# Four-layer graph network on one core: in layer 3 the exponent as a maximum of a copied row and a column, the division on ScalarE, the residual on GpSimd

## The chip, the cores and the metric

The kernel runs on one core of a Trainium2 chip. A core has five engines that run side by side and wait for each other through semaphores: TensorE (PE, matrix products and transposes into PSUM), VectorE (DVE), ScalarE (ACT, functions with a scale and a bias per partition), GpSimd (POOL) and SyncE (SP, which issues DMAs). Time is device microseconds (us) of one execution; the number of a kernel is the median of its runs.

## The reference, cut to what matters

Four layers follow each other on x of shape 16 batches x 512 nodes x 128 features; after each one, `x = layernorm(x + layer(x))`. The change is nearly all in layer 3, a graph attention with one head:

```python
Wh = einsum('bnf,fo->bno', h, W)
s1 = Wh @ a1;  s2 = Wh @ a2
e = s1[:, :, None] + s2[:, None, :]
e = where(e >= 0, e, 0.2 * e)
e = where(adj_matrix == 0, -inf, e)
attention = softmax(e, axis=-1)
h_prime = einsum('bij,bjo->bio', attention, Wh)
x = layernorm(x + h_prime)
```

Layer 0 is a linear recurrence of eight steps (folded into products with powers of a matrix L), layer 1 a normalised aggregation with two small products and batch norms, layer 2 a masked attention with four heads.

## The kernel before, in words

Everything stays in SBUF: m.X holds all 16 batches. Each layer is a software pipeline over batches (layer 0: pairs of batches). A step of the pipeline is a list of items per engine; an item with stage k works on batch s - k in step s. `pairs` writes out the first and last steps and runs the rest in a loop, two steps a turn. Each engine runs its list strictly in order, and an item waits for the semaphores it needs. So the order strings set the schedule. Between layers 2 and 3 the steps of both are interleaved by hand in strings called `tail`, where "E4.15" is item E4 of layer 2 for batch 15 and "3q0.0" is item q0 of layer 3 for batch 0.

Layer 3, for one batch (tile k of 128 source nodes j on the partitions, 512 target nodes i along the row):

- PE: x (4 transposes), w0 w1 (Wh and its columns times a), j (row of s2 for the masked maximum), i (row of s1, the same in all partitions), q0 to q3 (mask plus a row with minus the maximum, through the diagonals dg, in banks 4 and 5), a0 to a3 (attention times Wh, banks 6 and 7; column 0 of Wh is one, so it gives the denominator).
- DVE: m0 to m3 (maximum over the masked row of s2), c0 c1 (the row maximum e_max from it, tiles em), e0 to e3 (the exponent: bank + S2_SLOPE column + rl), d0 d1 (reciprocal), r0 to r3 (bank x reciprocal + X, into the tile r, "rc" in the trace), b (bn_stats), B (bn_aggr).
- ACT: XR, X (copies of the transposed x), W0 W1 (copies of Wh), G (four diagonals dg from the identity), L0 to L3 (relu of 0.8 (s1 + s2)), E0 E1 (exponential over two tiles each).
- POOL: copy of X into Xc for the transposes (`pool_copy`), the root of the variance and the four applications of the layernorm (`pool_norm`). SP then stores the batch (`sync`).

The leaky relu is 0.2 e + relu(0.8 e). Tiles are double buffered by the parity of the batch: rc for batch b is free when the store of batch b - 2 has landed (`stored[par]` in item r); item W waits for av (all a of batch b - 2); item a0 waits for all exponentials of its batch and for r0, r1 of the batch before. In layer 2, the item c2 (rb = bank x reciprocal) waits for y of the batch before, since rb has one buffer; S0 to S3 on POOL make half sums for D0 D1 on PE.

## Time and profile before

| | |
|---|---|
| time, median of 3 runs | 944.48 us (944.11 to 945.14) |
| the profiled execution | 941.33 us, of it a span of 939.5 us |
| busy, share of the span | PE 92%, DVE 67%, ACT 54%, POOL 43% |
| layer 3, 850 to 900 us | of 50 us: PE 48.0, DVE 46.3, ACT 41.9, POOL 28.8 |
| granted TensorE clock | 0.987 over the span, 1.00 between 800 and 900 us |

The profile gives busy times per engine, a timeline of instructions with the idle time before each and what ended it, and the chain of waits that ended last. Layer 0 fills the span to about 343 us, layer 1 to 445 us, layer 2 to 795 us, and layer 3 the rest. A share over the whole span says little here: each layer has its own pipeline and its own bound.

### The profile page before, as it was taken

What the parts mean: (1) busy time and instruction counts of PE and PEld (TensorE: products, weight loads), DVE (VectorE), ACT (ScalarE), POOL (GpSimd) and SP (SyncE); (2) the same over time, 40 slices, a digit from 0 to 9 for tenths busy, and PEclk for the clock granted to TensorE, in tenths of its full rate; (3) what the DMA queues carried; (4) which work ended last, traced back from release to release, by engine and by line L of the source; (5) the groups of instructions that cost most, each with busy time, mean ns of one, the idle gap of its engine ahead of it and who ended that gap; (6) DMA issues with size and microseconds to landing.
All of it is one profiled execution on the core that took longest, in us unless ns stands there. A gap on an engine that the chain in (4) does not pass through costs nothing. (4 is left out here: it accounts for less than half of the span.)

```text
span 939.5 us, 20538 instructions
## 1 busy us (share of the span) xinstructions
...
## 2 busy tenths in 40 slices
...
DMA packets 34249, 40.82 MB, mean 43 GB/s; under 512 B 6673, under 2 KB 17553, under 8 KB 34193
## 3 DMA queue, kind: packets, MB, share of 16 engines
...
## 5 line engine op out<-in xcount | busy, mean ns | idle before, releaser
L1678 POOL TENSOR_TENSOR half_sum<-prob 128x1024 f32<-128x1024 f32 x64 | 151.4, 2378 | 21.6 <-PE bank L1942 20.3
L1753 ACT ACTIVATE prob<-wide 128x1024 f32<-128x1024 f32 x128 | 124.2, 1023 | 38.3 <-PE wide L1934 38.1
L458 ACT CAST yT<-wide 128x512 fp32r<-128x512 f32 x48 | 28.1, 588 | 190.9 <-PE wide L862 141.9
L1822 DVE CUSTOM_DVE_ANT_0 junk<-wide,mask_ij 128x512 bf16<-128x512 f32 x128 | 82.7, 684 | 52.1 <-PE bank L1914 51.0
L1930 PE MATMUL wide<-qk_st 128*128 128x512 f32 x256 | 84.5, 435 | 3.2 <-ACT prob L1753 1.7
L1822 DVE CUSTOM_DVE_ANT_0 junk<-bank,mask_ij 128x512 bf16<-128x512 f32 x128 | 83.0, 685 | 0.0
L551 POOL TENSOR_TENSOR Xr<-Xf,Xr 128x512 fp32r<-128x512 f32 x16 | 20.4, 1291 | 140.1 <-ACT Xr L453 139.9
L1488 PEld LDWEIGHTS bank<-Wh,pr 128*128 128x128 f32 x512 | 65.2, 191 | 15.6 <-ACT pr L1341 7.0
L1488 PE MATMUL bank<-Wh,pr 128*128 128x129 f32 x512 | 68.5, 278 | 6.4 <-ACT pr L1341 5.5
L59 PE MATMUL bank<-z,L3T_hi 128*128 128x256 f32 x256 | 72.6, 284 | 1.3 <-DVE z L675 1.3
L61 PE MATMUL bank<-z,L3T_lo 128*128 128x256 f32 x256 | 72.3, 283 | 0.0
L60 PE MATMUL bank<-z,L3T_hi 128*128 128x256 f32 x256 | 72.3, 282 | 0.0
L1930 PEld LDWEIGHTS wide<-qk_st 128*128 128x128 f32 x256 | 46.4, 192 | 30.2 <-DVE mx L1822 19.2
L154 POOL TENSOR_SCALAR n_rstd<-n_aggr 128x4 f32<-128x4 f32 x31 | 7.2, 233 | 135.7 <-DVE n_aggr L147 130.3
L1952 PE MATMUL bank<-prob,v 128*32 128x512 f32 x512 | 61.6, 598 | 1.2 <-ACT prob L1753 1.2
L661 DVE TENSOR_TENSOR yT<-wide,yT 128x512 fp32r<-128x512 f32 x48 | 32.9, 686 | 31.8 <-ACT yT L458 31.8
L59 PEld LDWEIGHTS bank<-z,L3T_hi 128*128 128x128 f32 x256 | 48.7, 190 | 3.4 <-DVE z L675 2.6
L684 DVE TENSOR_TENSOR zf<-bank,G 128x256 f32<-128x256 f32 x64 | 27.0, 421 | 33.7 <-PE bank L61 32.0
L1914 PEld LDWEIGHTS wide<-qkT 32*128 32x128 f32 x128 | 12.3, 184 | 56.2 <-ACT prob L1753 29.6
L60 PEld LDWEIGHTS bank<-z,L3T_hi 128*128 128x128 f32 x256 | 48.8, 191 | 0.4
L61 PEld LDWEIGHTS bank<-z,L3T_lo 128*128 128x128 f32 x256 | 48.9, 191 | 0.0
L1377 DVE SCALAR_TENSOR_TENSOR pr<-bank,Wh,rl 128x512 f32<-128x512 f32 x64 | 44.9, 741 | 5.9 <-PE bank L1500 5.4
...
## 6 DMA issues: line engine op xcount, KB each, us to landing
...
qk_st<-neg_row SPq DMA_DIRECT2D x64, 2.0 KB
...
```

Of the source, the lines that this page charges most:

```text
L59: pe.matmul(out, stat[0], mov[0], start=start, stop=False)
L60: pe.matmul(out, stat[0], mov[1], start=False, stop=False)
L61: return pe.matmul(out, stat[1], mov[0], start=False, stop=stop)
L458: act.copy(yT[bb][i][0][:], psum_y[i][:]).then_inc(y_hi, 1)
L661: dve.tensor_tensor(yT[bb][i][1][:], psum_y[i][:], yT[bb][i][0][:].bitcast(F32), ALU.subtract).then_inc(y_lo, 1)
L1377: dve.scalar_tensor_tensor(out=pr[par][:, k], in0=bank[4 + k % 2][:], scalar=Wh[par][:, k, S2_SLOPE:S2_SLOPE + 1], in1=rl[par][:, k], op0= ...
L1488: last = pe.matmul(out_bank[h][:, t * (D + 2):t * (D + 2) + D + 1], pr[par][:, j, k * P:k * P + P], Wh[par][:, j, 0:D + 1], start=(j == 0) ...
L1678: pool.tensor_tensor(flat(half_sum[h][:]), flat(prob[bp][h][:, 0:2]), flat(prob[bp][h][:, 2:4]), ALU.add).then_inc(h_sum, 1)
L1753: act.activation(flat(prob[bp][h][:, 2 * half:2 * half + 2]), wide[half][:], ACT.Exp, scale=SCALE).then_inc(t_exp, 1)
L1822: dve.tensor_tensor_reduce(out=junk[h % 2][:], in0=ROWS[h][:], in1=m.mask_ij[:, i], scale=1.0, scalar=3.0 * MASKED, op0=ALU.add, op1=ALU.m ...
L1930: pe.matmul(bank[j][:], k_st[:, k, j * P:j * P + P], q_st[:, k], start=True, stop=True)
L1952: last = pe.matmul(ring["V0"][c, :], v[bp][:, k, c], prob[bp][h][:, k], start=(k == 0), stop=(k == NT - 1), skip_group_check=True)
```

## The change

In layer 3, the leaky relu is written as max(0.8 s1, -0.8 s2) + (mask and row) and s2 comes in as the bias of the exponential. e is then max(s1, 0.2 s1 - 0.8 s2) + s2 up to the row's own terms. The items become:

- ACT: L is gone; Z copies the s1 row from bank 1 to SBUF once per batch; E0 to E3 are four exponentials of one tile each, with the bias S2; R0 to R3 multiply bank 6 or 7 by the reciprocal into a new tile y; G is gone.
- DVE: e reads the copied row, the column S2_BEND and the bank (maximum, then addition); G (four products of the identity with em) is now on DVE; r is gone but for the last two batches; b and B have stage 3 in place of 2.
- POOL: `pool_add` adds y and X into rc, one instruction per batch with stage 4; the layernorm has stage 5 in place of 3.
- The s1 row always uses bank 1; the tile rl (and its place over qkT) is gone.
- The order strings of the transition from layer 2 to 3 change on PE, ACT, DVE and POOL.
- In layers 0 and 1, DVE's orders for the last steps of layer 0 change, its last two looped steps are written out, POOL makes the low part of batch 4 earlier, and DVE's statistics of the hidden layer start later.

```diff
-        LAST = ... "DVE": order("N z z z z A p p #a0 p #w0 p z z z z p p p p #a1 n #W0 #v0 a"),
-        LATE = ... "DVE": order("#a2 N A")}
+        LAST = ... "DVE": order("z z z z A p p #a0 p #w0 p z z z z p p p p #a1 n #W0 #v0 a"),
+        LATE = ... "DVE": order("#a2 N #a3 A")}
+        WHOLE = ... "DVE": order("h h y z z N y z z y A p p g p g g p g y z z y z z y p p g g n p p M g g a")}
...
                 if alive[2]:
                     for u in range(2):
+                        if u == 1 and isinstance(s, int) and s == groups + 1:
+                            batch_low(4, 0)
                         norm.root(pool, (s - 2 + CREDIT) * 2 + u, u)
...
-    ACT_ORDER = staged("L3:2 E0:2 W0:1 W1:1 E1:2 XR:0 G:1 L0:1 L1:1 X:0 L2:1")
-    DVE_ORDER = staged("m0:0 m1:0 d0:2 e0:1 e1:1 r0:2 m2:0 e2:1 e3:1 m3:0 r1:2 d1:2 c0:0 c1:0 r2:2 r3:2 b:2 B:2")
+    ACT_ORDER = staged("E0:2 E1:2 E2:2 W0:1 W1:1 E3:2 XR:0 Z:1 R2:3 R3:3 X:0 R0:2 R1:2")
+    DVE_ORDER = staged("m0:0 m1:0 d0:2 e0:1 e1:1 m2:0 e2:1 e3:1 d1:2 m3:0 c0:0 c1:0 G:0 b:3 B:3")
...
+    def late(b):
+        return isinstance(b, int) and b >= LAST - 1
...
+    def pool_add(pool, b, par, nth):
+        pool.wait_ge(res, after(b, NT))
+        pool.wait_ge(stored[par], (nth + 1) * 16)
+        pool.tensor_tensor(flat(r[par][:]), flat(y[par][:]), batch_flat(m.X, b), ALU.add).then_inc(summed, 1)
+
     def pool_rest(pool):
         def step(s, par, alive, nth):
             if alive[0]:
                 pool_copy(pool, s, par)
-            pool_norm(pool, s - 3, 1 - par, s if alive[0] else B - 1)
+            if alive[5]:
+                pool_norm(pool, s - 5, 1 - par, s if alive[0] else B - 1)
+            if alive[4] and not late(s - 4):
+                pool_add(pool, s - 4, par, nth - 2)
...
+            elif what == "Z":
+                act.wait_ge(s1_ps, after(b, 1))
+                act.wait_ge(e_s, after(b - 2, NT))
+                act.copy(s1[par][:], bank[1][:]).then_inc(s1_c, 1)
+            elif what == "R":
+                if late(b):
+                    return
...
+                act.activation(y[par][:, k], out_bank[h][:, t * (D + 2) + 1:t * (D + 2) + D + 1], ACT.Copy,
+                               scale=rec[par][:, k:k + 1]).then_inc(res, 1)
             elif what == "E":
-                two = flat(pr[par][:, 2 * k:2 * k + 2])
-                act.activation(two, two, ACT.Exp).then_inc(ex, 1)
+                act.activation(pr[par][:, k], pr[par][:, k], ACT.Exp,
+                               bias=Wh[par][:, k, S2:S2 + 1]).then_inc(ex, 1)
...
-                dve.scalar_tensor_tensor(out=pr[par][:, k], in0=bank[4 + k % 2][:],
-                                         scalar=Wh[par][:, k, S2_SLOPE:S2_SLOPE + 1], in1=rl[par][:, k],
-                                         op0=ALU.add, op1=ALU.add).then_inc(e_s, 1)
+                dve.scalar_tensor_tensor(out=pr[par][:, k], in0=s1[par][:],
+                                         scalar=Wh[par][:, k, S2_BEND:S2_BEND + 1], in1=bank[4 + k % 2][:],
+                                         op0=ALU.max, op1=ALU.add).then_inc(e_s, 1)
...
+            elif what == "G":
+                dve.wait_ge(e_m, after(b, 2))
+                dve.wait_ge(r_ps, after(b - 2, NT))
+                for t in range(NT):
+                    dve.tensor_scalar(dg[par][:, t], m.identb[:], em[par][:, 1, t:t + 1], None, ALU.mult).then_inc(d_g, 1)
             elif what == "d":
...
+                if isinstance(b, int) and b == LAST - 1:
+                    item(f"r{2 * k}", b, par, nth)
+                    item(f"r{2 * k + 1}", b, par, nth)
...
     def dve_last(dve, item):
+        item("b", LAST - 1, 0, LAST // 2)
+        item("B", LAST - 1, 0, LAST // 2)
...
-            tail("g2.13 S0.15 S1.15 S2.15 r.14 S3.15 g2.14", POOL_ORDER, work, None)
+            tail("g2.13 S0.15 S1.15 S2.15 S3.15 r.14 g2.14", POOL_ORDER, work, None)
...
-                 "E2.15 E3.15 f.14 3W1.0 E4.15 E5.15 e.14 E6.15 E7.15 3G.0 3L0.0 3L1.0 y.13 3XR.1 3L2.0 3L3.0 3X.1 f.15 e.15 "
-                 "3E0.0 3W0.1 3W1.1 y.14 3E1.0 3XR.2 3G.1 3L0.1 3L1.1 3X.2 3L2.1 y.15", ACT_ORDER, work, item)
+                 "E2.15 E3.15 f.14 3W1.0 e.14 y.13 E4.15 E5.15 E6.15 E7.15 3XR.1 3X.1 f.15 3Z.0 e.15 "
+                 "3E0.0 3E1.0 3W0.1 3W1.1 3E2.0 3E3.0 3XR.2 3Z.1 y.14 3X.2 3R0.0 3R1.0 y.15", ACT_ORDER, work, item)
```

The scales of the columns change with the formula, PE's items keep their sizes, and no DMA is added or removed.

The next two pieces are DVE's instructions in layer 3 behind its loop, from the last looped step on: first the kernel before. The tiles rc_4756 and rc_4757 belong to even and odd batches, so rc_4757 is batch 13 and then 15, rc_4756 batch 14; the pr rows are e of batch 15.

```order
L1393 RECIPROCAL rec_4765<-bank 128x2
L1377 SCALAR_TENSOR_TENSOR pr_4768<-bank,Wh_4750,rl_4760 128x512 x2
L1401 SCALAR_TENSOR_TENSOR rc_4756<-bank,rec_4765,X 128x128
L1377 SCALAR_TENSOR_TENSOR pr_4768<-bank,Wh_4750,rl_4760 128x512 x2
L1401 SCALAR_TENSOR_TENSOR rc_4756<-bank,rec_4765,X 128x128
L1393 RECIPROCAL rec_4765<-bank 128x2
L1401 SCALAR_TENSOR_TENSOR rc_4756<-bank,rec_4765,X 128x128 x2
L141 BN_STATS n_stats<-rc_4756 128x6 x4
L147 BN_AGGR n_aggr<-n_stats 128x2 x4
L1393 RECIPROCAL rec_4766<-bank 128x2
L1401 SCALAR_TENSOR_TENSOR rc_4757<-bank,rec_4766,X 128x128 x2
```

And the changed kernel at the same place, where rc_4732 is even and rc_4733 odd:

```order
L1418 RECIPROCAL rec_4743<-bank 128x2
L1429 SCALAR_TENSOR_TENSOR rc_4732<-bank,rec_4743,X 128x128 x2
L1397 SCALAR_TENSOR_TENSOR pr_4746<-s_row_4738,Wh_4726,bank 128x512 x4
L1418 RECIPROCAL rec_4743<-bank 128x2
L1429 SCALAR_TENSOR_TENSOR rc_4732<-bank,rec_4743,X 128x128 x2
L142 BN_STATS n_stats<-rc_4733 128x6 x4
L148 BN_AGGR n_aggr<-n_stats 128x2 x4
L142 BN_STATS n_stats<-rc_4732 128x6 x4
L148 BN_AGGR n_aggr<-n_stats 128x2 x4
L1418 RECIPROCAL rec_4744<-bank 128x2
L1429 SCALAR_TENSOR_TENSOR rc_4733<-bank,rec_4744,X 128x128 x2
```

r0 and r1 of batch 14 now stand ahead of all four e of batch 15, and the statistics of batch 13, which stood inside the loop, stand behind them.

The next two are POOL behind its loop: first the kernel before, which has the layernorm of batch 13 (rc_4757) and the roots of 14 and 15 left.

```order
L154 TENSOR_SCALAR n_rstd<-n_aggr 128x4
L156 TENSOR_TENSOR n_rstd<-n_rstd,neg_half 128x4
L182 TENSOR_SCALAR rc_4757<-rc_4757,n_aggr,n_rstd 128x128 x4
L154 TENSOR_SCALAR n_rstd<-n_aggr 128x4
L156 TENSOR_TENSOR n_rstd<-n_rstd,neg_half 128x4
```

And the changed kernel, in whose rows batch 11 comes first, with y_4735 and y_4736 the quotients from ScalarE:

```order
L183 TENSOR_SCALAR rc_4733<-rc_4733,n_aggr,n_rstd 128x128 x4
L1306 TENSOR_TENSOR rc_4732<-y_4735,X 128x512
L155 TENSOR_SCALAR n_rstd<-n_aggr 128x4
L157 TENSOR_TENSOR n_rstd<-n_rstd,neg_half 128x4
L183 TENSOR_SCALAR rc_4732<-rc_4732,n_aggr,n_rstd 128x128 x4
L1306 TENSOR_TENSOR rc_4733<-y_4736,X 128x512
```

The sum of batch 12 stands behind the layernorm of batch 11, and the sum of batch 13 behind the layernorm of batch 12.

The last two are ACT in the transition from layer 2 to layer 3, around y.14, the row with X<-rb; first the kernel before, from e.15 on:

```order
L1763 COPY denT<-bank 128x512
L1341 ACTIVATE pr_4767<-pr_4767 128x1024
L1323 COPY Wh_4750<-wide 128x2x131 x2
L175 ACTIVATE X<-rb,n_shift,n_rstd 128x128 x4
L1341 ACTIVATE pr_4767<-pr_4767 128x1024
L1314 CAST xTr_4751<-wide 128x512
```

And the changed kernel from e.15 on:

```order
L1792 COPY denT<-bank 128x512
L1362 ACTIVATE pr_4745<-pr_4745,Wh_4725 128x512 x2
L1344 COPY Wh_4726<-wide 128x2x131 x2
L1362 ACTIVATE pr_4745<-pr_4745,Wh_4725 128x512 x2
L1335 CAST xTr_4727<-wide 128x512
L1349 COPY s_row_4738<-wide 128x512
L176 ACTIVATE X<-rb,n_shift,n_rstd 128x128 x4
```

y.14 has moved behind the last exponential of batch 0, the cast XR.2 and the copy Z.1.

## Rows read from the trace of the kernel before

**Rows 1.** Busy time by window, layer 3: window, length, then busy us per engine.
```profile
850.00:900.00 50.00, 48.03 (x323) 37.29 (x321) 46.34 (x168) 41.90 (x83) 28.81 (x41) 1.00 0.11 31
```
**Rows 2.** Timeline of PE, layer 3: start us, us, engine line op, [idle before <-releaser].
```profile
819.04 0.66 PE L1450 MATMUL wide<-ident,Xc 128*128 128x128 f32 x4
820.08 1.16 PE L1488 MATMUL bank<-Wh,pr 128*128 128x129 f32 x8 [0.38 <-ACT pr L1341]
...
922.04 2.05 PE L1488 MATMUL bank<-Wh,pr 128*128 128x129 f32 x16 [0.84 <-ACT pr L1341]
```
**Rows 3.** Timeline of DVE over one step of layer 3, b of one batch to the next.
```profile
811.77 0.87 DVE L141 BATCH_NORM_STATS2 n_stats<-rc 128x6 f32<-128x128 f32 x4
...
819.03 0.15 DVE L1383 SCALAR_TENSOR_TENSOR em<-Wh,mx 128x4 f32<-128x4 f32 x1
819.22 0.16 DVE L1388 SCALAR_TENSOR_TENSOR em<-mx,em 128x4 f32<-128x4 f32 x1
819.50 0.61 DVE L1401 SCALAR_TENSOR_TENSOR rc<-bank,rec,X 128x128 f32<-128x128 f32 x2
820.14 0.87 DVE L141 BATCH_NORM_STATS2 n_stats<-rc 128x6 f32<-128x128 f32 x4
```
**Rows 4.** Timeline of POOL: an addition of layer 2, then layer 3.
```profile
801.45 1.27 POOL L1684 TENSOR_TENSOR rb<-rb,X 128x512 f32<-128x512 f32 x1 [6.69 <-DVE rb L1835]
...
818.25 0.61 POOL L1267 COPY Xc<-X 128x512 f32 x1 [0.25 <-POOL rc L182]
821.77 0.19 POOL L154 TENSOR_SCALAR n_rstd<-n_aggr 128x4 f32<-128x4 f32 x1 [2.91 <-DVE n_aggr L147]
...
823.28 3.12 POOL L182 TENSOR_SCALAR rc<-rc,n_aggr,n_rstd 128x128 f32<-128x128 f32 x4 [0.21 <-POOL n_rstd L156]
```
**Rows 5.** Timeline of DVE, layers 0 and 2, narrow windows.
```profile
351.90 1.17 DVE L182 TENSOR_SCALAR X<-zf,n_aggr,n_rstd 128x128 f32<-128x128 f32 x1 [1.66 <-POOL n_rstd L156]
352.99 1.32 DVE L182 TENSOR_SCALAR X<-zf,n_aggr,n_rstd 128x128 f32<-128x128 f32 x1
802.50 0.24 DVE L1383 SCALAR_TENSOR_TENSOR em<-Wh,mx 128x4 f32<-128x4 f32 x1
```
**Rows 6.** Timeline of POOL at the first two of these.
```profile
351.71 1.26 POOL L556 TENSOR_TENSOR Xa<-X,Xa 128x512 fp32r<-128x512 f32 x1
352.94 1.28 POOL L556 TENSOR_TENSOR Xa<-X,Xa 128x512 fp32r<-128x512 f32 x1
```
**Rows 7.** Instructions of line 182: duration ns min/median/max.
```profile
L182 DVE TENSOR_SCALAR X<-zf,n_aggr,n_rstd x64: 333/341/1323, 106.1 to 354.5; 128x128 f32<-128x128 f32 x32, 128x128 f32 x32
```
**Rows 8.** Groups of instructions, 850 to 900 us: count, busy us, mean ns, idle us.
```profile
L1330 ACT ACTIVATE rl<-wide,Wh 128x512 f32<-128x512 f32 x23 | 14.7, 697 | 0.0
```
**Rows 9.** Timeline of the end, DVE and POOL.
```profile
922.43 0.87 DVE L141 BATCH_NORM_STATS2 n_stats<-rc 128x6 f32<-128x128 f32 x4
931.63 0.61 DVE L1401 SCALAR_TENSOR_TENSOR rc<-bank,rec,X 128x128 f32<-128x128 f32 x2 [1.20 <-DMA out_dram<-rc]
...
925.54 3.12 POOL L182 TENSOR_SCALAR rc<-rc,n_aggr,n_rstd 128x128 f32<-128x128 f32 x4 [0.21 <-POOL n_rstd L156]
```
**Rows 10.** Timeline of PE at the seam of layers 0 and 1.
```profile
326.85 0.39 PE L59 MATMUL bank<-z,L3T_hi 128*128 128x256 f32 x1 [0.96 <-DVE z L675]
353.04 0.50 PE L59 MATMUL wide<-AhT_hi,Xa 128*128 128x512 f32 x1 [1.50 <-POOL Xa L556]
357.94 0.49 PE L59 MATMUL bank<-agT,W1T 128*128 128x512 f32 x1 [1.84 <-DVE agT L650]
```
**Rows 11.** Timeline of PE, DVE and ACT at the seam of layers 2 and 3.
```profile
785.82 1.92 PE L1952 MATMUL bank<-prob,v 128*32 128x512 f32 x16
...
791.82 3.33 PE L1942 MATMUL bank<-half_sum,ones_hd 128*32 128x512 f32 x16 [3.64 <-POOL half_sum L1678]
800.55 0.69 DVE L1835 TENSOR_TENSOR rb<-bank,rec 128x512 f32<-128x512 f32 x1 [0.60 <-ACT X L175]
798.77 1.65 ACT L175 ACTIVATE X<-rb,n_shift,n_rstd 128x128 f32<-128x128 f32 x4
```

More of the change, by code:

```diff
@@ L80, in setup_constants, with pairs @@
     m.AhT = [sb("AhT_hi", [P, NT, N], F32R), sb("AhT_lo", [P, NT, N], F32R)]
-def pairs(eng, steps, depth, step, first=0, last=None):
+def pairs(eng, steps, depth, step, first=0, last=None, loop_to=None):
     def alive(s):
@@ L92, in pairs @@
         step(s, s % 2, alive(s), s // 2)
-    with eng.Fori(lead // 2, steps // 2) as r:
+    loop_to = steps if loop_to is None else loop_to
+    with eng.Fori(lead // 2, loop_to // 2) as r:
         for parity in range(2):
             step(r * 2 + parity, parity, [True] * depth, r)
-    for s in range(steps, steps + depth - 1 if last is None else last + 1):
+    for s in range(loop_to, steps + depth - 1 if last is None else last + 1):
         step(s, s % 2, alive(s), s // 2)
@@ L587, in _ @@
             pairs(pool, groups, 5, step)
-            for b in range(4, 6):
-                batch_low(b, b - 4)
+            batch_low(5, 1)
             pool.wait_ge(la_x_lo, after(5, 1))
@@ L805, in step, with hidden_statistics @@
                                                  op1=ALU.subtract).then_inc(v_Ah, 1)
-            pairs(dve, groups, 5, step)
+            pairs(dve, groups, 5, step, loop_to=groups - 2)
+            def hidden_statistics(b):
+                for c in range(CH):
+                    dve.wait_ge(la_h_sb, after(b, CH, c + 1))
+                    dve.bn_stats(L1.st1[:, c, bass.ds(b, 1)].rearrange("p a n -> p (a n)"),
+                                 Hb[:, bass.ds(b, 1), c].rearrange("p a n -> p (a n)")).then_inc(la_h_st, 1)
             def aggregate_step(s, par, alive, nth):
-                early = isinstance(s, int) and s < 4
-                if alive[1] and not early:
+                if alive[1]:
                     aggregate_low(s - 1, 1 - par)
                 if alive[2]:
-                    b = s - 2
-                    for c in range(CH):
-                        dve.wait_ge(la_h_sb, after(b, CH, c + 1))
-                        dve.bn_stats(L1.st1[:, c, bass.ds(b, 1)].rearrange("p a n -> p (a n)"),
-                                     Hb[:, bass.ds(b, 1), c].rearrange("p a n -> p (a n)")).then_inc(la_h_st, 1)
-            pairs(dve, B, 5, aggregate_step)
+                    hidden_statistics(s - 2)
+            for b, behind in ((4, (0,)), (5, (1, 2)), (6, (3, 4)), (7, (5, 6)), (8, (7,))):
+                aggregate_low(b, b % 2)
+                for k in behind:
+                    hidden_statistics(k)
+            pairs(dve, B, 3, aggregate_step, first=10)
         @block.tensor
@@ L1138, in staged, with layer3 @@
     return [(word.split(":")[0], int(word.split(":")[1])) for word in text.split()]
-def layer3(nc, own, m, bank, out, rl1_at, ready):
+def layer3(nc, own, m, bank, out, ready):
     at = [172352]
@@ L1167, in layer3 @@
     onesb = over("onesb", [P, P], BF16)
-    rl = [over("rl0", [P, NT, N]), nc.alloc_sbuf_tensor_at("rl1", [P, NT, N], F32, offset=rl1_at)]
+    y = [over(f"y3{k}", [P, NT, D]) for k in range(2)]
+    s1 = [over(f"s1_row{k}", [P, N]) for k in range(2)]
     mx = [over(f"mx3{k}", [P, NT]) for k in range(2)]
@@ L1211, in half, with rest_of @@
         return bank[4 + k] if is_batch(b, 0) else bank[0] if k else bank[3]
-    def s1_bank(b):
-        return bank[4] if is_batch(b, 0) else bank[1]
+    def late(b):
+        return isinstance(b, int) and b >= LAST - 1
+    def rest_of(b, k):
+        return (late_res, (b - LAST + 1) * NT + k) if late(b) else (res, after(b, NT, k))
     def in_order(item, items):
@@ L1402, in item @@
                                          scalar=rec[par][:, k:k + 1], in1=tile_of(m.X, b, k),
-                                         op0=ALU.mult, op1=ALU.add).then_inc(res, 1)
+                                         op0=ALU.mult, op1=ALU.add).then_inc(late_res, 1)
             elif what == "b":
-                dve.wait_ge(res, after(b, NT))
+                if late(b):
+                    dve.wait_ge(*rest_of(b, NT))
+                else:
+                    dve.wait_ge(summed, after(b, 1))
                 norm.statistics(dve, b + CREDIT, par, r[par])
@@ L1446, in item @@
                 if is_batch(b, 1):
-                    pe.wait_ge(*ready["second wide"])
+                    pe.wait_ge(*ready["first two"])
                 pe.wait_ge(wh_c, after(b - 1, 2))
@@ L1485, in item @@
                 for j in range(NT):
[L1486 to L1487 removed]
+                    if one_by_one and j >= 1:
+                        pe.wait_ge(ex, after(LAST, NT, j + 1))
                     last = pe.matmul(out_bank[h][:, t * (D + 2):t * (D + 2) + D + 1],
```

96 lines of the change are left out of this document (41 added, 55 removed).

## The prediction

> **What bounds the kernel now.** I read the busy times by window first, then the timeline of one step of layer 3 on each engine, then the two seams between layers, and last the chain at the end.
>
> In layer 3 no engine is far from full [rows 1]: PE 48.0 of 50 us, DVE 46.3, ACT 41.9. A step is one batch. From the start of a0 at 820.08 to the start of a0 of batch 14 at 922.04 [rows 2] there are 12 steps, so 8.50 us each. PE is idle in each step before a0, 0.30 to 0.38 us (0.38 in the row shown), until ACT has done the double exponential. Ahead of that it waits for W1 before x, which does not change. So PE could go at about 8.50 - 0.34 = 8.16 us if the exponentials came sooner.
>
> DVE is nearly as full: from b of one batch at 811.77 to b of the next at 820.14 [rows 3] are 8.37 us without a gap, and behind it DVE waits a little for j. That is the engine that the change relieves, and it moves work to POOL, which works 28.8 of 50 us.
>
> **The change part by part.**
>
> *Seam of layers 0 and 1.* PE stands three times [rows 10]. At 326.85 it waits 0.96 us for z, since the statistics N stand ahead of z on DVE. They move into the step before (M), where DVE waits for PE anyway: -0.9. At 353.04 PE waits for the low part of batch 4, which POOL makes at 351.71 [rows 6] behind two roots. It now stands between them: the wait of 1.50 us goes. At 357.94 it waits 1.84 us for agT, which stood on DVE behind the four applications A and four statistics. It now stands ahead of both. The time goes whole, since PE stands nowhere else near: 4.3, and with the pipeline's refill of some 0.1 to 0.2 at each of them 4.6 us. If one of the inputs is late for another reason, 3. I take -4.6.
>
> *Seam of layers 2 and 3.* PE waits 3.64 us at 791.82 for the last half sum, and the 16 products behind the wait take 3.33 us, where 16 of the same width at 785.82 take 1.92 [rows 11]. The half sum S3.15 now stands ahead of r.14, and D0.14 ahead of t2.15. The wait and the slow products go: up to 3.64 + 1.41, less 0.2 for the s1 row's product and the exponentials that move: -4.8. Against it stands y.14. At 798.77 it ran between the two exponentials of batch 0 [rows 11], and c2.15 on DVE waits for it (0.60 us at 800.55). Now it stands behind E2.0, E3.0, XR.2 and Z.1, four instructions of ScalarE at some 0.6 to 0.7 us each [rows 8]: 2.6 later. Behind c2.15 on DVE are queued m2.1 and m3.1, for which j.2 on PE waits, and then a1.0 and q0.1, so PE stands at j.2. y.15 also comes ahead of the exponentials of batch 1. Together +3.0. The sum of this seam is -1.8, between -4.8 (y.14 costs nothing) and +1.
>
> *Relu, division, residual in the steady loop, if nothing gets in the way.* ACT loses four relus of 0.70 us [rows 8] and four diagonals, gains one copy of a row and four products of 128 columns, and its exponentials come one tile at a time. Then a0 waits for a single tile behind W1, and the idle time before a0 goes: 8.16 us a step. I cost e at the same time as before, since it still reads one bank, one SBUF tile and one column. DVE loses four r, two of which take 0.64 us from 819.50 to b at 820.14 [rows 3]: -1.28, leaving 7.09. It gains four G of 128 bf16 columns. No row shows one; bounds are c0's 0.15 (4 columns) and r's 0.32 (128 columns): 0.6 to 1.3 us a step, so 7.7 to 8.4. POOL gains one sum of 128x512, as that at 801.45: 1.27 us [rows 4]. Its own chain per batch, counted from the start of b: root at 821.77 - 820.14 = 1.63, the four applications from 3.14 to 6.26, then 0.25 (as before the copy at 818.25), the sum from 6.51 to 7.78, and b of the next batch may start. 7.8 is under 8.16.
>
> *DVE and POOL at the same moment.* The trace shows them in each other's way. At 351.71 POOL begins an instruction of 1.26 us, ending at 352.97. DVE's tensor_scalar of 128 columns, issued at 351.90, ends at 353.07, 0.10 after it. The next is issued at 352.99, POOL's next runs from 352.94 to 354.22, and DVE's ends at 354.31 [rows 5, 6]; the median of these instructions is 0.34 us [rows 7]. Of the kind of c0, one at 802.50 takes 0.24 in place of 0.15 [rows 3, 5], and it ends at 802.74, where POOL's sum from 801.45 ends at 802.72 [rows 4]. In the loop before, c0 and c1 fell into POOL's idle time, and no instruction of G's kind was there. The Trainium skill says the same in "SBUF — State Buffer", section "Who interferes with whom": a DVE instruction with two SBUF inputs, or in a two-port mode, and a GpSimd instruction lock each other out for a whole instruction. By that rule, the trace agrees.
>
> Where does c0 fall now? Counted from b: 819.03 - 811.77 = 7.26 in the row, less two r (0.64), is 6.62. The sum on POOL runs from 6.51 to 7.78. So c0 is held until 7.78. c1 follows 0.19 later and G 0.28 after that [rows 3], at 8.25. By then POOL's copy has begun (7.78 + 0.25 = 8.03, for 0.61 [rows 4]), so G starts at 8.64, and four take 0.6 at the 0.15 that I take for one (bounds 0.15 and 0.32): b at 9.24 (to 9.9). As b starts POOL's next chain, this repeats in every step, whatever its length: 9.24 us in place of 8.16. If G does not need what POOL holds, it goes from 8.25 on, and the step has 8.9 to 9.5 all the same. The rule of "VectorE: DVE Perf Modes", section "The TRN2 errata", gives 58 + FD/4 cycles, an estimate of 0.09 us for one G; the step would have 9.0.
>
> From a0.1 to a0.14 are 13 steps: two before the first sum meets a c0, then eleven. 13 x (8.16 - 8.50) = -4.4, and 11 x (9.24 - 8.16) = +11.9: +7.5.
>
> *The end.* Before, b of batch 13 starts at 922.43, its applications end at 928.66, and r0 of batch 15 waits for the landed store until 931.63 [rows 9]; from there to the end of the span are 7.87. From a0.14 at 922.04 it is 17.46 in all. Now b has stage 3, and POOL does the sum of batch 13 only behind the applications of batch 12. b of batch 12 starts about 1.3 us behind a0.14 (0.8 without the collision). From there: 6.26 to the end of its applications, 2.97 for the store (931.63 - 928.66), and only then may r0 of batch 14 write, which stands ahead of e of batch 15: 9.2. Then r0 and r1 (0.6), four e, d1, r2 and r3 of 14: 4.2 more, of which the e are some 0.7 each. b of batch 13 starts at 13.4 to 14; 6.26 and 2.97 again to r0 of batch 15: 22.9. I take 22.1, since the e may overlap with the store's last part. The end is 7.87 behind. Sum 1.3 + 22.1 + 7.87 = 31.3 against 17.46: +13.8. Nothing hides it: all other engines have finished by then.
>
> **The sum.** -4.6 - 1.8 + 7.5 + 13.8 = +14.9. The profiled execution took 941.33, so 956.2; the median is 3.15 above the profiled execution, so 959.4 us.
>
> **The rivals.**
>
> *The engines do not collide in the loop* (the sum and c0 miss each other, or c0 is not held). For it: only one c0 in the trace is held, and it was a tenth of a microsecond. Against: the margin from 6.51 to 7.78 is wide, and DVE's next instruction would fall in it too. Then the step has 8.16 and the end 0.5 less: -4.6 - 1.8 - 4.4 + 13.3 = +2.5, 947.0 us.
>
> *It is faster.* The same, and PE fills entirely: with ACT emptier W1 comes sooner, the further stall before x goes, and y.14 costs nothing. From x at 819.04 to a0 at 820.08 are 1.04 us [rows 2], of which x itself needs 0.5, so 0.54 a step with no stall at all: 13 x 0.54 = 7.0. -4.6 - 4.8 - 7.0 + 13.3 = -3.1, 941.4 us. It decides if DVE's step stays under 7.9, which needs every c and G free of POOL. Against it: the end alone takes all that back.
>
> *The end is milder.* If the stores land well before r0.14 and r0.15, the end costs some 5 in place of 13.8, with the collision in the loop: 950.6 us. The chain of applications, store and r at 931.63 speaks against it.
>
> *Collision with a slow G* of 0.32: 9.9 a step, +7.3 more, 966.7 us.
>
> **How the numbers follow.** Forecast 0.55 (own range 953 to 965), no collision 0.2, milder end 0.1, slow G 0.07, faster 0.08. What a measurement can tell from no change is 0.2%, 1.9 us. No collision at 947.0 with 3 us around lies half over 946.4 and half in or under it. So slower 0.83, same 0.08, faster 0.09. The range, 945 to 966, leaves out the faster case and the far ends.
>
> **What would show it.** In the changed kernel's profile: PE without idle time at 326, 353 and 358 us; D of batch 15 without a wait, and PE idle at j.2 instead. In the loop, a0 to a0 at 9.2 us, PE's busy share in layer 3 falling to about 7.9 of 9.2, and em and dg instructions on DVE ending together with POOL's sum and copy. At the end, two waits of DVE for a store, at r of batch 14 and of 15. I am wrong if a0 to a0 stays under 8.5, or if DVE does not wait for a store ahead of batch 15's e.

## The result, and the profile after

The changed kernel takes 957.11 us (median of 4 runs, 955.41 to 957.61), the kernel before on the same chip 944.3. The ratio is 1.0134, 95% interval 1.0116 to 1.0152: slower by 1.2 to 1.5%. The forecast was 959.4. By the medians the change costs 12.8 us.

The profiled execution took 957.17 us, with a span of 955.3; before, 941.33 and 939.5. The one before was 3 us faster than its median and this one was not, so the difference of the two spans, 15.8 us, holds some 3 us of spread between executions. It falls into four parts, read from three places that both traces have: the residual c2.12 late in layer 2 (the rb row on DVE), the start of a0 of batch 1, and the start of a0 of batch 14.

| stretch | before | after | difference | forecast |
|---|---|---|---|---|
| start to c2.12 (seam 0/1) | 751.32 | 746.39 | -4.9 | -4.6 |
| c2.12 to a0.1 (seam 2/3) | 60.2 | 62.1 | +1.9 | -1.8 |
| a0.1 to a0.14 (13 steps) | 110.5 | 114.4 | +3.9 | +7.5 |
| a0.14 to the end | 17.5 | 32.4 | +14.9 | +13.8 |

The rows of these places, first DVE of the kernel before, then DVE and PE of the changed kernel (timelines: start us, us, engine line op):

```profile
751.32 0.69 DVE L1835 TENSOR_TENSOR rb<-bank,rec 128x512 f32<-128x512 f32 x1
```
```profile
746.39 0.69 DVE L1864 TENSOR_TENSOR rb<-bank,rec 128x512 f32<-128x512 f32 x1
...
808.53 1.16 PE L1519 MATMUL bank<-Wh,pr 128*128 128x129 f32 x8
...
922.93 2.05 PE L1519 MATMUL bank<-Wh,pr 128*128 128x129 f32 x16 [0.53 <-ACT pr L1362]
```

Busy times by window of the changed kernel. The three stops of [rows 10] are gone: PE is busy 50.00 of 50 us in both windows of the first seam. Layer 3, against [rows 1], has less on PE (46.6 for 48.0) and on ACT (33.5 for 41.9), more on POOL (33.4 for 28.8), and as much as before on DVE.

```profile
300.00:350.00 50.00, 50.00 (x312) 45.97 (x311) 27.73 (x93) 14.29 (x31) 11.08 (x13) 1.00 0.04 6
350.00:400.00 50.00, 50.00 (x216) 40.28 (x215) 26.78 (x45) 28.86 (x48) 20.17 (x16) 1.00 0.00 0
...
850.00:900.00 50.00, 46.62 (x307) 35.34 (x306) 46.12 (x159) 33.54 (x74) 33.35 (x44) 1.00 0.11 31
```

*The second seam*, PE, DVE and ACT of the changed kernel, against [rows 11] (L1959 t3.15, L1971 D of batch 15, L1519 a0.0, L1864 c2.15, L176 y.13 and y.14, L1782 the exponentials E4.15 and E5.15):

```profile
776.56 2.04 PE L1959 MATMUL wide<-qk_st 128*128 128x512 f32 x4 [2.66 <-ACT prob L1782]
...
787.15 1.92 PE L1971 MATMUL bank<-half_sum,ones_hd 128*32 128x512 f32 x16
...
797.94 2.06 PE L1519 MATMUL bank<-Wh,pr 128*128 128x129 f32 x8 [3.84 <-DVE rb L1864]
...
797.10 0.69 DVE L1864 TENSOR_TENSOR rb<-bank,rec 128x512 f32<-128x512 f32 x1 [3.23 <-ACT X L176]
...
772.96 1.65 ACT L176 ACTIVATE X<-rb,n_shift,n_rstd 128x128 f32<-128x128 f32 x4
774.51 1.91 ACT L1782 ACTIVATE prob<-wide 128x1024 f32<-128x1024 f32 x2
...
795.31 1.65 ACT L176 ACTIVATE X<-rb,n_shift,n_rstd 128x128 f32<-128x128 f32 x4
```

D of batch 15 has no wait and takes 1.92 in place of 3.33, as forecast. But a0.0 now stands 3.84 us for c2.15, which stands 3.23 for y.14; the forecast had this stop at j.2. And there is a place that the forecast didn't have: t3.15, the last scores of layer 2, stands 2.66 us for the exponentials E4.15 and E5.15, ahead of which y.13 runs on ACT from 772.96.

*One step of layer 3*, DVE and then POOL, against [rows 3, 4]:

```profile
851.40 1.01 DVE L1403 SCALAR_TENSOR_TENSOR em<-Wh,mx 128x4 f32<-128x4 f32 x1
852.45 0.16 DVE L1408 SCALAR_TENSOR_TENSOR em<-mx,em 128x4 f32<-128x4 f32 x1
852.65 0.74 DVE L1414 TENSOR_SCALAR dg<-identb,em 128x128 bf16<-128x128 bf16 x4
853.31 0.87 DVE L142 BATCH_NORM_STATS2 n_stats<-rc 128x6 f32<-128x128 f32 x4
...
860.69 0.68 DVE L1403 SCALAR_TENSOR_TENSOR em<-Wh,mx 128x4 f32<-128x4 f32 x1
...
862.25 0.87 DVE L142 BATCH_NORM_STATS2 n_stats<-rc 128x6 f32<-128x128 f32 x4
...
850.58 1.27 POOL L1306 TENSOR_TENSOR rc<-y,X 128x512 f32<-128x512 f32 x1
851.79 0.61 POOL L1280 COPY Xc<-X 128x512 f32 x1
854.90 0.20 POOL L155 TENSOR_SCALAR n_rstd<-n_aggr 128x4 f32<-128x4 f32 x1 [2.50 <-DVE n_aggr L148]
...
856.42 3.14 POOL L183 TENSOR_SCALAR rc<-rc,n_aggr,n_rstd 128x128 f32<-128x128 f32 x4 [0.21 <-POOL n_rstd L157]
859.52 1.27 POOL L1306 TENSOR_TENSOR rc<-y,X 128x512 f32<-128x512 f32 x1
860.74 0.61 POOL L1280 COPY Xc<-X 128x512 f32 x1
```

c0 does the same work as before, on 4 columns, where it took 0.15 us. The one issued at 851.40 ends at 852.41, the one at 860.69 at 861.37; POOL's copies end at 852.40 and 861.35. G is not held: four take 0.74. From b to b are 8.94 us.

*The end*, DVE and then POOL, against [rows 9]:

```profile
923.91 0.86 DVE L142 BATCH_NORM_STATS2 n_stats<-rc 128x6 f32<-128x128 f32 x4
...
932.82 0.61 DVE L1429 SCALAR_TENSOR_TENSOR rc<-bank,rec,X 128x128 f32<-128x128 f32 x2 [7.37 <-DMA out_dram<-rc]
...
938.58 0.86 DVE L142 BATCH_NORM_STATS2 n_stats<-rc 128x6 f32<-128x128 f32 x4
...
947.43 0.61 DVE L1429 SCALAR_TENSOR_TENSOR rc<-bank,rec,X 128x128 f32<-128x128 f32 x2 [6.10 <-DMA out_dram<-rc]
...
927.03 3.14 POOL L183 TENSOR_SCALAR rc<-rc,n_aggr,n_rstd 128x128 f32<-128x128 f32 x4 [0.21 <-POOL n_rstd L157]
...
941.69 3.13 POOL L183 TENSOR_SCALAR rc<-rc,n_aggr,n_rstd 128x128 f32<-128x128 f32 x4 [0.21 <-POOL n_rstd L157]
```

DVE stands twice for a landed store, 7.37 us ahead of r0.14 and 6.10 ahead of r0.15, where before it stood 1.20. From b.12 to r0.15 are 23.5 us.

### The profile page after: what moved, and what is told of

Its sections match the earlier page's. It is cut to its first block and busy times, and to the rows that moved or that the text cites. A ratio compares the mean times of both kernels' runs of the same rounds, so it can differ in the third digit from the quotient of the medians.

```text
span 955.3 us, 20263 instructions
## 1 busy us (share of the span) xinstructions
PE 870.6 (91%) x6039; PEld 624.0 (65%) x6039; DVE 629.3 (66%) x1939; ACT 485.2 (51%) x878; POOL 420.9 (44%) x465
## 3 DMA queue, kind: packets, MB, share of 16 engines
q1 hardware_dynamic: 32816, 39.87, 17.4%
## 5 line engine op out<-in xcount | busy, mean ns | idle before, releaser
L1782 ACT ACTIVATE prob<-wide 128x1024 f32<-128x1024 f32 x128 | 124.1, 1022 | 38.5 <-PE wide L1963 38.4
L1959 PE MATMUL wide<-qk_st 128*128 128x512 f32 x256 | 84.8, 437 | 5.9 <-ACT prob L1782 4.3
L1519 PEld LDWEIGHTS bank<-Wh,pr 128*128 128x128 f32 x512 | 69.0, 201 | 14.4 <-issue 6.8
L1519 PE MATMUL bank<-Wh,pr 128*128 128x129 f32 x512 | 71.9, 288 | 4.6 <-DVE rb L1864 3.8
L1959 PEld LDWEIGHTS wide<-qk_st 128*128 128x128 f32 x256 | 46.7, 194 | 32.9 <-DVE mx L1851 18.5
L1362 ACT ACTIVATE pr<-pr,Wh 128x512 f32<-128x512 f32 x64 | 45.1, 724 | 19.7 <-DVE pr L1397 19.5
```

The costliest lines, as they stand in the source:

```text
L1362: act.activation(pr[par][:, k], pr[par][:, k], ACT.Exp, bias=Wh[par][:, k, S2:S2 + 1]).then_inc(ex, 1)
L1519: last = pe.matmul(out_bank[h][:, t * (D + 2):t * (D + 2) + D + 1], pr[par][:, j, k * P:k * P + P], Wh[par][:, j, 0:D + 1], start=(j == 0) ...
L1782: act.activation(flat(prob[bp][h][:, 2 * half:2 * half + 2]), wide[half][:], ACT.Exp, scale=SCALE).then_inc(t_exp, 1)
L1959: pe.matmul(bank[j][:], k_st[:, k, j * P:j * P + P], q_st[:, k], start=True, stop=True)
```

## The experiments

Each ratio is to the kernel before, run on the same chip; the median of the kernel before was 942.7 to 944.0 beside these runs. The changed kernel was not run beside them. So "under the changed kernel" means under its median of 957.11, measured at another time; taken from the ratios, the same gains are smaller: 10.7 us for 12.2, 8.2 for 9.7, 8.4 for 9.5 and 2.8 for 3.3. The traces stand nearer to the smaller figures, as said at each. The theory was: DVE and POOL collide at c0 in every step, and the end is a chain through two stores.

**Own buffers at the end.** Batches 14 and 15 get tiles for the result and the aggregates, where qkT lay.

```diff
-                dve.scalar_tensor_tensor(out=r[par][:, k], in0=out_bank[h][...],
+                dve.scalar_tensor_tensor(out=r_late[par][:, k], in0=out_bank[h][...],
...
-                    dve.wait_ge(stored[par], (nth + 1) * 16)
+    aggr_late = [... offset=late_at + (2 + k) * NT * D * 4 ...]
```

> The changed kernel, with a result buffer and an aggregate of their own for batches 14 and 15, so that r0.14 and r0.15 need no landed store of batches 12 and 13. Theory (the longer end is the chain of applications, store, r, twice): DVE does r0.14 right behind d0.14, b.13 starts behind the sum of batch 13, and from a0.14 to the end of the span it takes about 20 to 21 us in place of 32.4: 957.1 - 12 = 945 us (943 to 947). The loop stays at 8.96 a step. Rival (the end is long because the products and exponentials of batch 15 come late, or because b has stage 3, and the stores only happen to land there): under 4 us are gained, 953 or more.

944.92 us (943.30 to 947.16), ratio 1.0021 [0.9999, 1.0042]: 12.2 under the changed kernel, as the theory had it. From a0.14, at 920.13, to the end of the span, 941.5, are 21.4 us, 11.0 less than in the changed kernel; the rest of the difference lies ahead of a0.14, where these buffers are not used. Both waits for a store are gone; what is left ahead of b.13 is 1.55 us for POOL's sum:

```profile
922.69 0.61 DVE L1440 SCALAR_TENSOR_TENSOR r_late<-bank,rec,X 128x128 f32<-128x128 f32 x2
...
928.65 0.87 DVE L142 BATCH_NORM_STATS2 n_stats<-rc 128x6 f32<-128x128 f32 x4 [1.55 <-POOL rc L1318]
```

The edit leaves the loop as it was, and yet the collision looks different in every second step. DVE, then POOL:

```profile
849.35 0.47 DVE L1415 SCALAR_TENSOR_TENSOR em<-Wh,mx 128x4 f32<-128x4 f32 x1
849.85 0.52 DVE L1420 SCALAR_TENSOR_TENSOR em<-mx,em 128x4 f32<-128x4 f32 x1
...
848.53 1.27 POOL L1318 TENSOR_TENSOR rc<-y,X 128x512 f32<-128x512 f32 x1
```

This c0 was issued 0.82 us into the sum, as the one at 851.40 in the changed kernel was. Here it ends with the sum (849.82 and 849.80), and c1 is held by the copy in its place; there it was held through the copy. c0 takes 577 ns on average of eight (850 of nine in the changed kernel), and the eleven steps up to a0.14 take 8.82 us each in place of 8.90. What decides between the two is not shown.

**POOL's sum first.**

```diff
+            if alive[4] and not late(s - 4):
+                pool_add(pool, s - 4, par, nth - 2)
             if alive[5]:
                 pool_norm(pool, s - 5, 1 - par, s if alive[0] else B - 1)
-            if alive[4] and not late(s - 4):
-                pool_add(pool, s - 4, par, nth - 2)
```

> The changed kernel, with POOL's sum of a batch ahead of the root and the applications of the batch before it, in place of behind them. Nothing else moves. Theory (a closed loop: B on DVE releases the root on POOL, 1.5 us; applications 3.14, sum 1.27, copy 0.61 follow without a gap, c0 of DVE is held till the copy's end, then c1, G, b, B: 8.96): the sum now runs beside b and B, the copy ends before c0 is issued, c0 takes 0.15 again, and the step falls to 8.2 to 8.3, where PE bounds it: 13 x 0.65 = 8.5 us less, about 949 us (947 to 951). Rival (a step is long because DVE has G, the new e and c0 to do, and c0's duration is only idle time shown as work): within 2 us of 957.

957.35 us (955.39 to 962.01), ratio 1.0163 [1.0110, 1.0216]. No gain: the forecast of 949 fell. The trace, POOL and DVE, says why:

```profile
858.66 0.61 POOL L1280 COPY Xc<-X 128x512 f32 x1 [0.24 <-POOL rc L183]
861.13 1.27 POOL L1306 TENSOR_TENSOR rc<-y,X 128x512 f32<-128x512 f32 x1 [1.86 <-DMA out_dram<-rc]
```
```profile
857.98 0.16 DVE L1403 SCALAR_TENSOR_TENSOR em<-Wh,mx 128x4 f32<-128x4 f32 x1
858.18 0.16 DVE L1408 SCALAR_TENSOR_TENSOR em<-mx,em 128x4 f32<-128x4 f32 x1
858.37 1.11 DVE L1414 TENSOR_SCALAR dg<-identb,em 128x128 bf16<-128x128 bf16 x4
```

The sum has to wait for the store of the batch two before, which the old place hid: 1.86 us idle, and the root of the next applications stands behind it. So POOL's chain slid by about as much as was won. c0 is nearly free (0.16 here, 0.33 to 0.35 in three of the later steps), but the copy now falls on G, 1.11 for 0.74. The step is 8.67 on average of eleven (823.59 to 919.00) rather than 8.2, which wins 2.5 us on the changed kernel, and the end, with applications of batch 12 behind such a sum, gave the rest back: from b.12 at 919.80 to r0.14 at 931.03 are 11.2 in place of 8.9. So the first part of the theory held (what POOL does when c0 comes sets c0's time), and the price of the move had been left out.

**Sum and copy in four instructions each.**

```diff
-        pool.tensor_tensor(flat(r[par][:]), flat(y[par][:]), batch_flat(m.X, b), ALU.add).then_inc(summed, 1)
+        for t in range(NT):
+            last = pool.tensor_tensor(r[par][:, t], y[par][:, t], tile_of(m.X, b, t), ALU.add)
+        last.then_inc(summed, 1)
```

> The changed kernel, with POOL's sum and copy of a batch in four instructions of 128 columns each. The work and the order are the same. Theory (DVE's c0 waits for the end of the one instruction that POOL has under way): c0 takes at most 0.35 in place of up to 1.0 and no longer waits for the last of them; the step falls by 0.3 to 0.6, so 950 to 954 us. G may now meet parts of the copy, each 0.15. Rival (c0 waits for POOL's whole batch of work, or the duration comes from something else): c0 stays at 0.6 to 1.0 and the time at 957.

962.85 us (960.51 to 965.09), ratio 1.0202 [1.0153, 1.0252]: slower still, against the forecast. The edit does not leave POOL's time alone, as the expectation had it: from the start of the sum to the end of the copy are 2.64 us (863.12 to 865.76), where one instruction each took 1.83 (859.52 to 861.35). Of the 6.3 us by which the spans differ, 1.4 lie between a0.1 and a0.14, 2.7 at the end and 2.2 ahead of a0.1. POOL, then DVE:

```profile
863.12 1.69 POOL L1312 TENSOR_TENSOR rc<-y,X 128x128 f32<-128x128 f32 x4
864.76 1.00 POOL L1284 COPY Xc<-X 128x128 f32 x4
```
```profile
864.27 1.50 DVE L1410 SCALAR_TENSOR_TENSOR em<-Wh,mx 128x4 f32<-128x4 f32 x1
865.80 0.16 DVE L1415 SCALAR_TENSOR_TENSOR em<-mx,em 128x4 f32<-128x4 f32 x1
```

c0 starts at 864.27, in the third of the four sums, and ends at 865.77, when the last of four copies has ended (865.76). It was passed over at five boundaries between POOL's instructions. In the step before it was issued just ahead of such a boundary and ended with the next instruction, after 0.48. The ten steps alternate: five c0 take 1.49 to 1.69 and end with the copy, five take 0.48 to 0.49. So c0 does not always get in when the one instruction under way ends; in half of the steps it waits until POOL's whole run of instructions has ended. In the changed kernel the c0 of 851.40 comes during a sum and leaves behind the copy, too.

**G back on ScalarE.**

```diff
-    DVE_ORDER = staged("... m3:0 c0:0 c1:0 G:0 b:3 B:3")
+    DVE_ORDER = staged("... m3:0 c0:0 c1:0 b:3 B:3")
-    ACT_ORDER = staged("... E3:2 XR:0 Z:1 ...")
+    ACT_ORDER = staged("... E3:2 XR:0 G:1 Z:1 ...")
```

> The changed kernel, with the four diagonals G back on ScalarE (behind the copy XR, as in the kernel before; POOL's order stays). Theory (closed loop of 8.96 through POOL): c0 is held just as long, but the loop loses G's 0.66 between c1 and b: 8.30 a step, so about 8 us less, 949 us (947 to 951), with c0 still at 0.6 to 1.0. Rival 1 (the price is G's alone, since DVE is full): c0 falls back to 0.15 and the step to the 8.16 of PE, 947 or less. Rival 2 (ScalarE becomes late with its products and exponentials): no gain, 955 or more.

947.44 us (946.58 to 949.63), ratio 1.0047 [1.0027, 1.0067]: 9.7 under the changed kernel; between a0.1 and a0.14 the trace has 7.3 us less. The time is near to rival 1, and so is c0, which is back at 0.16 to 0.21 (187 ns on average of nine): the theory's figure of 0.6 to 1.0 was wrong. Without G's 0.66 the loop has 8.30 us at most, PE has 8.2, and the two are so near that c0 comes just as the copy ends. The step is 8.25 (808.06 to 898.83 in eleven). The run does not part G's own time from the hold, since it removes both.

**b ahead of c0, c1, G.** This run leaves G on DVE: no work is added or moved to another engine.

```diff
-    DVE_ORDER = staged("m0:0 m1:0 d0:2 e0:1 e1:1 m2:0 e2:1 e3:1 d1:2 m3:0 c0:0 c1:0 G:0 b:3 B:3")
+    DVE_ORDER = staged("m0:0 m1:0 d0:2 e0:1 e1:1 m2:0 e2:1 e3:1 d1:2 m3:0 b:3 B:3 c0:0 c1:0 G:0")
```

> The changed kernel with one move on DVE: b and B of a batch ahead of c0, c1 and G, in place of behind them. Work and all other orders stay. Theory (c0 waits because POOL's sum and copy run back to back when it comes, and stands in the loop B, root, applications, sum, copy, c0, c1, G, b, B): c0 now comes 1.2 us later, when POOL has ended its copy, and is out of the loop through b; c0 takes 0.15 to 0.3, the step falls from 8.96 to 8.2 to 8.5, 6 to 9 us less, 948 to 951 us. G can be held by POOL's root (1.03) in some steps. Rival (q0 of the next step waits for G, which comes 1.2 later, so PE stands): the step stays at 8.9 or goes up, 956 or more.

947.61 us (946.27 to 948.46), ratio 1.0045 [1.0028, 1.0062]: 9.5 under the changed kernel, G still on DVE. Its windows row, then DVE and PE of one step:

```profile
850.00:900.00 50.00, 49.52 (x333) 39.19 (x339) 46.91 (x174) 37.03 (x80) 37.69 (x49) 1.00 0.11 31
```
```profile
857.45 0.16 DVE L1403 SCALAR_TENSOR_TENSOR em<-Wh,mx 128x4 f32<-128x4 f32 x1
857.65 0.16 DVE L1408 SCALAR_TENSOR_TENSOR em<-mx,em 128x4 f32<-128x4 f32 x1
857.85 0.75 DVE L1414 TENSOR_SCALAR dg<-identb,em 128x128 bf16<-128x128 bf16 x4
...
856.66 1.16 PE L1519 MATMUL bank<-Wh,pr 128*128 128x129 f32 x8
...
864.89 1.15 PE L1519 MATMUL bank<-Wh,pr 128*128 128x129 f32 x8
```

PE has no idle time before q or a0 any more, and from a0 to a0 are 8.18 us (807.61 to 897.59 in eleven). DVE has as much to do as in the changed kernel. These 13 steps (807.61 to 913.78) take 8.2 us less than in the changed kernel. So what the steady part lost came of the loop that the hold of c0 closed: b, root, applications, sum, copy, then c0, c1 and G, and b again. The move takes c1 and G out of that loop together with c0, so their shares are not measured apart; but G's 0.66 us, which DVE still has to do, cost nothing outside it. Rival: PE would stand for G. It does not.

**The seams.** First, the kernel before with the edits between layers 0 and 1 alone:

```diff
+        WHOLE = {"PE": ORDER, "ACT": ORDER, "DVE": order("h h y z z N y ... n p p M g g a")}
+                        if u == 1 and isinstance(s, int) and s == groups + 1:
+                            batch_low(4, 0)
```

> The kernel before with only the edits at the seam of layers 0 and 1 (statistics M a step earlier, low part of batch 4 between the two roots, agT ahead of the last applications, statistics of batches 0 to 7 beside the low parts). Theory: the three stops of PE of 0.96, 1.50 and 1.84 us go with their refill, 4.6 to 4.9 us less, about 938 (the before of this chip at 942.7), ratio 0.995, and all later parts of the trace stand the same time apart as in the kernel before. Rival (part of it is taken back at the start of layer 1, where something else is late): under 2 us, ratio over 0.998.

937.86 us (936.71 to 938.45), ratio 0.9933 [0.9910, 0.9957]: 4.1 to 8.5 us less. PE is full in both windows (50.00 of 50), and c2.12 comes at 747.63, 3.7 earlier. The rival is out; whether the seam is worth 3.7, 4.9 or 6 lies inside the spread of single traces.

Next, the kernel before with one swap on POOL:

```diff
-            tail("g2.13 S0.15 S1.15 S2.15 r.14 S3.15 g2.14", POOL_ORDER, work, None)
+            tail("g2.13 S0.15 S1.15 S2.15 S3.15 r.14 g2.14", POOL_ORDER, work, None)
```

> The kernel before with one swap on POOL: the half sum S3.15 ahead of the residual r.14. Theory: the residual waits for DVE until 788.1, so the half sum runs in that wait and ends some 3.3 us earlier; the idle 3.64 of PE ahead of D.15 and its slow 3.33 in place of 1.92 go, 3.5 to 4.8 us less, ratio about 0.996. Rival (the normalisation y.14 and c2.15 behind it are then what a0.0 waits for, since their chain starts at the residual, which now comes later): 0 to 1.5 us less.

938.51 us (937.07 to 940.90), ratio 0.9939 [0.9918, 0.9960]: 3.8 to 7.7 us less, so the rival (0 to 1.5) is out. D.15 on PE has 0.33 of its 3.64 idle left, and its normal 1.92:

```profile
790.09 1.92 PE L1942 MATMUL bank<-half_sum,ones_hd 128*32 128x512 f32 x16 [0.33 <-POOL half_sum L1678]
```

Last, the changed kernel with y.14 moved:

```diff
-                 "E2.15 E3.15 f.14 3W1.0 e.14 y.13 ... f.15 3Z.0 e.15 "
-                 "3E0.0 3E1.0 3W0.1 3W1.1 3E2.0 3E3.0 3XR.2 3Z.1 y.14 3X.2 3R0.0 3R1.0 y.15"
+                 "E2.15 E3.15 f.14 3W1.0 e.14 y.13 ... f.15 3Z.0 e.15 y.14 "
+                 "3E0.0 3E1.0 3W0.1 3W1.1 3E2.0 3E3.0 3XR.2 3Z.1 3X.2 3R0.0 3R1.0 y.15"
```

> The changed kernel with the normalisation y.14 on ScalarE moved ahead of the exponentials of batch 0, behind the copy e.15. Theory (c2.15 on DVE, and a0.0 on PE behind it, wait for y.14: 3.23 and 3.84 us in the changed kernel): c2.15 goes at about 793.7 in place of 797.1, a0.0 follows the last exponential, 3 us less, 954 us. Rival (the root of batch 14, or y.15 behind it, is late anyway): under 1 us less.

953.81 us (952.55 to 954.15), ratio 1.0104 [1.0080, 1.0128]: 3.3 less. DVE and PE:

```profile
794.21 0.69 DVE L1864 TENSOR_TENSOR rb<-bank,rec 128x512 f32<-128x512 f32 x1
```
```profile
795.05 1.13 PE L1519 MATMUL bank<-Wh,pr 128*128 128x129 f32 x8
```

c2.15 waits for nothing, a0.0 comes 2.9 earlier and at full clock.

On top of that, y.13 was moved too:

```diff
-                 "... e.14 y.13 E4.15 E5.15 E6.15 E7.15 ..."
+                 "... e.14 E4.15 E5.15 y.13 E6.15 E7.15 ..."
```

> The changed kernel with y.14 ahead of the exponentials of batch 0 (953.8), and y.13 on ScalarE behind E4.15 and E5.15 of layer 2 in place of ahead of them. Theory (the missing gain of the second seam: y.13, 1.65 us, stands ahead of E4.15, so the last scores product t3.15 stands 2.66 us on PE, PE's granted clock falls to 0.60 behind it and the four products take 2.04): the wait falls to 0.5 to 1.2 us, the products take 1.2, q0.0 comes 2 to 3 us earlier than its 789.25, and so does a0.1; about 951.5 us, ratio 1.008. Rival (E4.15 is not what counts, since POOL's half sums of batch 15 set D.15 and q0.0 behind it): t3.15 comes earlier, but D.15 stands longer, q0.0 within 0.7 us of 789.25, 953 to 954.

951.70 us (951.07 to 953.76), ratio 1.0098 [1.0078, 1.0119]: 2.1 less than with y.14 moved alone by the medians, 0.6 by the ratios, whose intervals overlap; the times alone do not show the gain. In the traces, q0.0 stands 13.1 us behind the last products of t2.15 (787.65 and 774.59; its own row is missing, and the time is that of the row behind it less the usual 0.22), and 15.7 without this move (789.25 and 773.58): 2.6 won, as forecast. The way was only half as forecast. The wait of t3.15 fell from 2.66 to 2.19, but its products ran at the full clock, in 1.16 us in place of 2.04:

```profile
777.22 1.16 PE L1959 MATMUL wide<-qk_st 128*128 128x512 f32 x4 [2.19 <-ACT prob L1782]
...
775.00:780.00 5.00, 2.59 (x37) 1.72 (x29) 0.46 (x2) 4.61 (x8) 5.00 (x3) 1.00 0.00 0
```

The granted clock from 775 to 780 us was 1.00, where the changed kernel had 0.60 there and 0.72 up to 785. So of the 2.6 us only 0.5 are the wait itself, and most of the rest is the clock. Why it stayed up behind a wait of 2.19 and fell behind one of 2.66 is not shown.

**Versions that beat both.** Three mends in the changed kernel, with G on ScalarE; then the kernel before with its two seams mended and its own layer 3; then three mends in the changed kernel that add no work.

> The changed kernel with three mends together: diagonals back on ScalarE, own buffers for batches 14 and 15, y.14 ahead of the exponentials of batch 0. If the gains add: 957.1 - 9 - 12 - 3 = 933 us, about 1% under the kernel before. If the end then has another limit (the exponentials and products of batch 15, at a lower clock of PE, in place of POOL's chain), 3 to 4 us less gain, 936 to 937. If they don't add at all, 944.

934.23 us (933.62 to 935.42), ratio 0.9902 [0.9871, 0.9933]. Taken from the ratios (8.2, 10.7 and 2.8), the three gains add to within 0.2 us; the differences of medians (9.7, 12.2 and 3.3) would have given 931.9.

> The kernel before, layer 3 as it was, with both mends of the seams: the edits between layers 0 and 1, and the half sum S3.15 ahead of the residual r.14. Theory (the seams are independent): 6.1 + 5.4 = 11.5 us under the kernel before, ratio 0.988, 932 to 933 us: as fast as the changed kernel with its three mends, so that the rewritten layer 3 brings nothing that its later end does not take. Rival (part of both gains is the same idle time, or the spread of the runs made them look large): 7 to 8 us less, ratio 0.992, and the rewritten and mended kernel stays ahead.

933.50 us (933.35 to 934.34), ratio 0.9895 [0.9878, 0.9911]: near to the forecast of 932 to 933, and clear of the rival's 0.992.

> The changed kernel with three mends that add no work: b and B ahead of c0, c1, G on DVE; own buffers for batches 14 and 15; y.14 ahead of the exponentials of batch 0. The division, G on DVE and the sum on POOL stay as in the change. If the three gains add (9.5, 12.2, 3.3): 932 us, ratio 0.988, the same as the kernel before with its two seams mended (933.5). If G on DVE lengthens the end where ScalarE's did not, 934 to 936.

931.70 us (931.24 to 932.90), ratio 0.9865 [0.9812, 0.9918], the lowest median of all. Its three gains would have given 932.1 by the medians; by the ratios 0.990, which its wide interval holds. Its window of layer 3, and its a0.14:

```profile
850.00:900.00 50.00, 49.88 (x339) 39.17 (x338) 46.83 (x171) 36.80 (x80) 37.85 (x50) 1.00 0.11 31
...
910.38 2.05 PE L1530 MATMUL bank<-Wh,pr 128*128 128x129 f32 x16 [0.51 <-ACT pr L1374]
```

So most of the gain over the kernel before is in the seams. The rewritten layer 3, with its order and its buffers right, has 13 steps in 106.2 us (a0.1 at 804.22) where the old one with the same seams has 111.5 (802.90 to 914.43), and an end of 19.8 in place of 17.4. That is 1.6 us in the profiled spans (930.2 and 931.8), while the intervals of the two ratios overlap: whether it is ahead at all is not shown. The move of y.13, 2.6 us in its own trace, was not tried on top.

## Why the prediction was right, step by step

- *Sign and size.* +15.8 in the profiled executions, +12.8 by the medians, +14.9 forecast. Two terms were off by 3.7 (seam 2/3) and by 3.6 (the loop), in opposite directions; the total owes its closeness to that, which is luck. The 3.15 us added from the profiled execution to the median did not hold for the changed kernel, whose profiled execution lay at its median.
- *Seam 0/1, -4.6.* -4.9 in the trace, 3.7 in the trace of the edits alone. Right; the refill of 0.1 to 0.2 at each stop, 0.3 us of the term, is less than these two differ by, so no run shows it.
- *Seam 2/3, -1.8.* +1.9, and outside its range of -4.8 to +1. D.15 lost its wait and its slow products as forecast, and y.14 cost 3.3 by the medians and 2.9 in the trace, forecast 3.0. It did so at another place: the forecast had PE stand at j.2, behind m2.1 and m3.1, and PE stood at a0.0, which waits for c2.15 itself. The step that failed is the 0.2 us taken for "the s1 row's product and the exponentials that move". q0.0 came 6.07 us earlier (789.01 for 795.08), of which 4.93 are the first seam's: 1.1 won and not 4.8. y.13 and e.14 stand ahead of E4.15 on ACT, so t3.15 waits 2.66 and then runs at a granted clock of 0.60, and putting y.13 back behind gives 2.6 us again. About 1 us of this term stays open: D0.14 and D1.14, now ahead of t2.15, should delay E4.15 as well, which was not tried.
- *Steady loop without a collision, 8.16 a step.* 8.18 when the collision is taken away, 8.22 in the first two steps of the changed kernel. Right.
- *The collision, 9.24 a step.* The mechanism is shown: c0 at up to 1.02 us, ending with POOL, in a loop that closes through b; moving c0, c1 and G out of it gives back 9.5 us by the medians, 8.2 in the traces. The size was off: 8.90 on average over the eleven steps (824.98 to 922.93), the last of which, behind a c0 of 0.16, took 8.1, so +3.9 and not +7.5. Two terms failed. The forecast put 0.25 us ahead of the sum and of the copy each, as the row of the copy had it [rows 4]; POOL ran applications, sum and copy without a gap. And it let c0 in between sum and copy and held G behind the copy; in this execution c0 was held through both, and G met nothing; with buffers of their own for batches 14 and 15, c0 did get in there in every second step, and c1 was held instead. From b, the copy ends at 8.04 (853.31 to 861.35), then c1, G and b: 8.94.
- *The end, +13.8.* +14.9, by the steps named: r0.14 8.9 behind b.12 (forecast 9.2), r0.15 23.5 behind it (22.1), the last part 7.87 as before. The 1.4 more lies between r0.14 and b.13, 5.76 us (932.82 to 938.58) where the forecast had 4.2 to 4.8. DVE stands 0.54 and 0.97 us there for PE's products, which ran at a granted clock of 0.50 to 0.52 (1.2 GHz, the lower level) from 934 to 940 us, after 7.49 us in which PE stood. And the 0.8 us taken off because "the e may overlap with the store's last part" could not come: all four e stand behind r0.14, which waits for that store. Two result tiles of 256 KB give back 12.2 by the medians, 11.0 at this place in the traces.
- *The rivals.* "No collision" (947.0) is out, by c0. "A milder end" is out, by the two waits. The slow G was not there: 0.25 us each by its row, but 0.17 from one to the next, near to the 0.15 taken. The Trainium skill's "VectorE: DVE Perf Modes", section "The TRN2 errata", gives an estimate of 0.09 us for one; the measured figure decides.
